# First layer's attention output by transfers instead of turns, parts sent by GpSimd, operands sent earlier

## The chip, the cores and the metric

The kernel runs on one core of a Trainium2 chip. The metric is the device time of one execution in microseconds (us); less is better. Five engines work side by side, each through its own list of instructions in order: TensorE (PE; its weight loads are shown as PEld), VectorE (DVE), ScalarE (ACT), GpSimd (POOL) and SyncE (SP), which here only starts transfers (DMAs). They meet through semaphores: an instruction may wait until a counter has reached a value.

## What is computed

Two transformer-like layers on `x` of 4 sequences, 512 tokens and 256 channels; 16 heads of 16 channels. All in float32 at the interface.

```python
# layer 0
xm = rmsnorm(x) * (1 + scale(cond)) + shift(cond)
q, k, v = split(xm @ w_qkv); q, k = rope(q), rope(k)
o = softmax(q @ k.T * DH ** -0.5) @ v            # per head
x = o @ w_out + x
# layer 1
xn = layer_norm(x)
q, k, v = xn @ q_w + q_b, xn @ k_w + k_b, (xn @ v_w + v_b) * mask
y = softmax(q @ k.T + (1 - mask) * -1e6) @ v     # per head
h = layer_norm(y) * (1 + scale(emb)) + shift(emb)
x = x + silu(h) @ out_w + out_b
```

## The kernel before

**Groups and steps.** The attention of one layer, one sequence and four heads is a group. There are 2 x 4 x 4 = 32 groups, 0 to 15 in layer 0 and 16 to 31 in layer 1. After an opening, the kernel runs one step for each group, s = 0 to 31. A step has four key tiles (k = 0 to 3) of 128 keys each. `KEY_TILE` (L43) is the order within a tile, by which every engine's list is written (`order`, L210): for each of the four heads a score product of 128 keys by 512 queries (L538), a second product that adds the row maximum with a minus sign (L550), and a product for the row maxima of the group two steps ahead (L559); and at the tile's end the product of the tile before with the values (`values`, L576), which adds up in one bank, `ACC`. ACT takes the exponentials (L765), DVE the row maxima (L938 in layer 0, L935 in layer 1), into three banks in turn (`ND = 3`). The maxima of a group are made into two float16 parts by DVE (`negate`, L946 and L948, up to group 21) or by POOL (from group 22), turned by PE in the second tile (L584), copied by ACT (L778), and written by SP into the operand of L550 (`shift`, L1443 to L1449).

**Pieces.** All other PE work is put into the middle of tiles as pieces, by the table `PIECES` (L91 to L115): `qk` and `v` are the projections (L626, L637), `y` is the output projection of a layer (L654, two for each sequence), `turn` is a transpose of normalised tokens to channels (L611, eight 128 x 128 transposes for a pair).

**Output of a group.** In the first tile of step s the last values product of group s-1 ends. ACT copies `ACC` to `oT` (L772): rows are channels of a head (16 of every 32), and one more row holds the sum of its probabilities. In the middle of tile k = 2 PE turns `oT` (four transposes, L591) into one of the DVE's three banks, and DVE writes `1 / sum` (L960) and the product (L962) into `O`, tokens by channels (`write_output`, L951). For layer 0, when the four groups of a sequence are done, `turn f0` turns `O` back to channels by tokens (L611, source `O`), ACT copies it into `xT` (L802), and `y(0, b)` reads it.

**Parts.** Queries and keys go through HBM. POOL splits each of four chunks of a sequence (unit `pu`, 0 to 3 in layer 0, 4 to 7 in layer 1) into two float16 parts (`rope`, L1210, of five instructions in layer 0; `split`, L1198, of two in layer 1). SP sends the parts, four transfers of 128 KB for a chunk, at the steps in `PARTS_AT` (L163), and loads a group's operands (L1431) three steps ahead. In step s SP's list is: `shift(s+1)`, `operands(s+3)`, then parts. Only unit 0 has transfers from POOL in the kernel before (L1276, L1278: ten). After the ropes of sequence 1 POOL waits for the mask's transfers (`mask_in`), which SP starts in step 0 behind parts, makes the mask's rows (L1307 to L1314), and then runs the ropes of sequences 2 and 3 one behind another.

**Second layer.** `project(b)` on POOL (L1332) makes the norm's factors, the normalised tokens (L910), adds the output bias (L1337), then splits and adds the values' bias (`add_bias`, L1229). Behind it POOL makes the norm of the last stage, `turn f1` reads that in tiles 0 and 1 of step 22.

Of the kernel before, what the change touches and what calls it, by code (L numbers as in the profile page):

```python
# [12 lines left out]
P = 128  # L13
# [8 lines left out]
G = 4  # L22
# [6 lines left out]
GROUPS = LAYERS * B * NG  # L29
UNIT = 64.0  # L30
# [88 lines left out]
for _b in range(B):  # L119
    STATISTICS[5 + NG * _b, 3] = ("p1", _b, 0)  # L120
    STATISTICS[6 + NG * _b, 0] = ("p1", _b, 1)
# [32 lines left out]
for _s in range(1, GROUPS - 2):  # L154
# [8 lines left out]
PARTS_AT = {-1: ((1, 0), (1, 1)), 0: ((1, 2), (1, 3)), 2: ((2, 0), (2, 1)), 3: ((2, 2), (2, 3)),  # L163
            5: ((3, 0), (3, 1)), 6: ((3, 2), (3, 3))}
for _b in range(B):
    PARTS_AT[8 + NG * _b] = ((B + _b, 0), (B + _b, 1))
    PARTS_AT[9 + NG * _b] = ((B + _b, 2), (B + _b, 3))

# [18 lines left out]
def key_tile(s, k):  # L187

    for op, h in KEY_TILE:
# [86 lines left out]

def await_shift(engine, q, n):
# [43 lines left out]
def build(nc, x, condT, mask, tables, vecs, w_cond, w_qkv, w_out, w_qkv1, v_b, emb_w, out_w, out_b, out):  # L321
# [4 lines left out]
    with ExitStack() as ctx:  # L326
# [12 lines left out]
        m.v_aug = [sb(f"v_aug{i}", [P, KT, H, W]) for i in range(VALUES)]  # L339
        m.probs = [sb(f"probs{i}", [P, G, 512]) for i in range(KT)]  # L340
# [48 lines left out]
        m.roped = [[sb(f"roped{e}{i}", [P, 512]) for i in range(2)] for e in range(2)]  # L389
        m.parts = sb("parts", [P, 2, 4, 512], F16)  # L390
# [4 lines left out]
        m.k_dram = nc.dram_tensor("k_parts", [LAYERS * B, H, 2, 2, DH, S], F16, kind="Internal").ap()  # L395

# [8 lines left out]
        q.acc_copied = sem("acc_copied")  # L405
        q.shift_high = sem("shift_high")
# [115 lines left out]
def tensor(nc, pe, m, q):  # L522
# [71 lines left out]
    def turn_tokens(piece):  # L594
        _, kind, b, h = piece
        bank = d_free(D[piece]) if for_dve(piece) else a_free(A[piece])
        if kind == "f0":
            pe.wait_ge(q.d_done, D["output", NG * b + NG - 1] + 1)
            src = m.O[b % 2]
        else:  # L600
            n = NORMAL.index((kind, b))
            src = m.XN[n % 2]
            if h == 0 and n == 0:
                pe.wait_ge(q.ident_made, 4)
                pe.wait_ge(q.xn0_made, TPB)
            elif h == 0 and n == len(NORMAL) - 1:
                pe.wait_ge(q.xn0_made, 2 * TPB)
            elif h == 0:
                pe.wait_ge(q.xn_made, TPB * n)
# [31 lines left out]
    def tokens_out(piece):  # L641
# [3 lines left out]
        if j == 0:  # L645
            pe.wait_ge(q.late_in, 64)
            if layer:
                pe.wait_ge(q.silu_made, CT * (b + 1))
            else:
                pe.wait_ge(q.a_done, turned(USES[use]))  # L650
# [104 lines left out]
def scalar(act, m, q):  # L755
# [12 lines left out]
    def copy_output(s):  # L768
        act.wait_ge(q.values_done, KT * (s + 1))
        if s:  # L770
            act.wait_ge(q.d_made, D["output", s - 1] + 1)
        act.activation(m.oT[:, :], m.ACC, ACT.Copy).then_inc(q.acc_copied, 1)  # L772
# [7 lines left out]
    def tokens(piece):  # L780
# [20 lines left out]
        if kind == "f0":  # L801
            act.activation(to, bank, ACT.Copy).then_inc(q.a_done, 1)  # L802
# [111 lines left out]
def vector(dve, m, q):  # L914
# [35 lines left out]

    def write_output(s):  # L951
        pu, g = divmod(s, NG)
        bank = made(D["output", s]).rearrange("p (t h w) -> p t h w", t=KT, h=G)
        if g == 0 and 2 <= pu < B + 2:
            dve.wait_ge(q.a_made, turned(("f0", pu - 2)))
        if g == 0 and pu >= B + 2:
            dve.wait_ge(q.xn_made, TPB * NORMAL.index(("f1", pu - 2 - B)))
        if s:
# [180 lines left out]
    for op, *at in order():  # L1139
        if op == "max":  # L1140
            maximum(*at)
            n, j, h = at
            if (j, h) == (KT - 1, MAXED[-1]) and n not in POOL_SHIFTS:
                negate(n)
        if op == "output":
# [26 lines left out]
def gpsimd(pool, m, q):  # L1172
# [24 lines left out]

    def split(pu, i):  # L1198
# [9 lines left out]
            .then_inc(q.part_pool, 1)  # L1208

# [334 lines left out]
```

## Time and profile before

| | |
|---|---|
| median of 3 runs | 509.46 us (509.26 to 510.74) |
| the profiled execution's own time | 511.63 us |
| its span, first to last instruction | 509.8 us |
| PE, busy share of the span | 97% |
| DVE | 80% |
| ACT | 68% |
| POOL | 45% |
| mean granted TensorE clock | 1.000 |
| chain that ended last: PE, DVE | 75%, 15% |
| time before step 0; steps 1 to 4; 5; 6 to 17; 18 to 21; from 22 on | 57.7; 52.9; 16.1; 178.3; 56.5; 134.4 us |

The last line is from the first score product of each step in the timeline; step 0 itself takes 13.9 us. A PE that is busy for 97% isn't at its peak for 97%: matmuls overlap, and their ends are modelled. So the timeline of PE is read by the starts: how far the first product of one tile is from the first of the next.

### The profile page before, as it was taken

Reading aid. Unit: us, or ns where it says so; the run is one execution under the profiler, and the core shown is the slowest. Engines: PE = TensorE matmul, PEld = TensorE weight load, DVE = VectorE, ACT = ScalarE, POOL = GpSimd, SP = SyncE. Lnnn points to the kernel's source line nnn. Section 1 sums busy time; section 2 is a strip of 40 time slices with the busy share of each in tenths; the row PEclk is TensorE's granted clock in tenths of the full one; section 3 lists DMA queues with packets and bytes.
Section 4 is the critical chain, followed back from the end, with each engine's and each line's share of the span. In section 5 each row is a group of like instructions: output and inputs, shape, how many; then the busy total and the mean of one; then the engine's idle time right before and its main releaser. Section 6 shows DMA issues by size and latency. Waiting matters only on the chain.

```text
span 509.8 us, 9780 instructions
## 1 busy us (share of the span) xinstructions
PE 496.1 (97%) x3301; PEld 187.0 (37%) x3301; DVE 406.4 (80%) x1046; ACT 348.7 (68%) x684; POOL 228.8 (45%) x267
## 2 busy tenths in 40 slices
PE   7999899999999999999999999999999999999997
PEld 3554323333433245333443344333433333332234
DVE  3767887998896788967898688977899999999324
ACT  2652467768577785867768676777778778777863
POOL 6479537999361320923136330643672045005401
PEclk9999999999999999999999999999999999999999
DMA  7773356341323033111321133210341112211011
GB/s 251 197 197 124 86 163 211 112 141 43 111 67 104 13 126 124 43 44 51 116 86 44 42 104 122 68 43 2 124 125 45 43 43 84 85 44 43 2 42 41
DMA packets 42217, 45.30 MB, mean 89 GB/s; under 512 B 4324, under 2 KB 40308, under 8 KB 41912
## 3 DMA queue, kind: packets, MB, share of 16 engines
q1 hardware_dynamic: 41400, 42.06, 27.0%
q0 software_dynamic: 480, 1.31, 1.0%
q10 hardware_dynamic: 288, 1.31, 0.8%
q8 instruction: 26, 0.43, 0.3%
q14 instruction: 23, 0.19, 0.1%
HBM read 25.52 MB, written 18.87 MB: 87 GB/s over the span
## 4 chain that ended last, share of the span: by engine, by line
PE 75%; DVE 15%; issue 3%; ACT 2%; DMA 2%; POOL 1%; SPq 1%; DVEq 0%; ACTq 0%; POOLq 0%
PE bank L576 18%; PE bank L626 12%; PE bank L559 11%; PE bank L550 9%; PE bank L538 8%; DVE masked L935 6%; PE bank L637 6%; DVE row_max L938 5%; PE bank L654 5%; PE bank L591 2%; PE bank L611 2%; ACT probs L765 2%; DMA k_s<-k_parts 2%; PE bank L584 1%; PE bank L712 1%
## 5 line engine op out<-in xcount | busy, mean ns | idle before, releaser
L765 ACT ACTIVATE probs<-bank 128x512 f32<-128x512 f32 x512 | 272.8, 600 | 82.1 <-PE bank L550 80.9
L559 PE MATMUL bank<-k_s,q_s 64*128 64x512 f16 x512 | 182.8, 382 | 4.0 <-DVE row_max L938 2.5
L938 DVE TENSOR_REDUCE row_max<-bank 128x1 f32<-128x512 f32 x256 | 162.5, 684 | 28.9 <-PE bank L559 27.7
L935 DVE CUSTOM_DVE_ANT_0 masked<-bank,mask_bias 128x512 bf16<-128x512 f32 x256 | 163.3, 687 | 13.4 <-PE bank L559 12.3
L538 PE MATMUL bank<-q_s,k_s 64*128 64x512 f16 x512 | 152.1, 381 | 0.9 <-ACT v_aug L842 0.5
L550 PE MATMUL bank<-shift,kx 64*128 64x512 f16 x512 | 148.9, 376 | 0.0
L576 PE MATMUL bank<-probs,v_aug 128*17 128x512 f32 x1024 | 135.4, 598 | 0.7 <-ACT probs L765 0.7
L559 PEld LDWEIGHTS bank<-k_s,q_s 64*128 64x128 f16 x512 | 46.0, 93 | 156.1 <-DVE row_max L938 68.4
L626 PE MATMUL bank<-xT,wqkv 128*128 128x512 f32 x128 | 61.7, 612 | 0.9 <-DVE xT L1064 0.6
L550 PEld LDWEIGHTS bank<-shift,kx 64*128 64x128 f16 x512 | 46.8, 95 | 31.7
L538 PEld LDWEIGHTS bank<-q_s,k_s 64*128 64x128 f16 x512 | 31.5, 94 | 13.1 <-ACT probs L765 8.0
L1205 POOL CAST parts<-plain 128x512 f16<-128x512 f32 x16 | 9.8, 611 | 52.2 <-ACT plain L823 52.2
L626 PEld LDWEIGHTS bank<-xT,wqkv 128*128 128x128 f32 x128 | 22.2, 189 | 29.5 <-issue 26.0
L1358 POOL TENSOR_SCALAR scaled<-row_max 128x16 f32<-128x16 f32 x10 | 2.6, 259 | 64.6 <-DVE row_max L935 40.5
L637 PE MATMUL bank<-wqkv,xT 128*128 128x256 f32 x128 | 31.3, 389 | 0.0
L1193 POOL TENSOR_SCALAR spread<-moments_p 128x4 f32<-128x4 f32 x4 | 0.9, 232 | 67.0 <-DVE moments_p L973 67.0
L576 PEld LDWEIGHTS bank<-probs,v_aug 128*17 128x17 f32 x1024 | 17.9, 95 | 33.6 <-issue 15.6
L654 PE MATMUL bank<-wo,xT 128*128 128x256 f32 x112 | 27.9, 392 | 0.0
L637 PEld LDWEIGHTS bank<-wqkv,xT 128*128 128x128 f32 x128 | 23.2, 190 | 8.6 <-issue 4.1
L1240 POOL TENSOR_SCALAR v_bias<-vb_row,vecs 128x256 f32<-128x256 f32 x16 | 14.8, 927 | 23.1 <-ACT v_tmp L837 22.3
L984 DVE TENSOR_TENSOR X<-bank,X 128x512 f32<-128x512 f32 x14 | 9.6, 687 | 18.8 <-PE bank L654 18.8
L654 PEld LDWEIGHTS bank<-wo,xT 128*128 128x128 f32 x112 | 20.1, 189 | 8.1 <-DVE row_max L938 2.5
(123 smaller groups left out, 499.4 us busy)
## 6 DMA issues: line engine op xcount, KB each, us to landing
q_s<-q_parts SPq DMA_DIRECT2D x32, 256.0 KB, 2.8
k_s<-k_parts SPq DMA_DIRECT2D x32, 256.0 KB, 3.1
q_parts<-parts SPq DMA_DIRECT2D x60, 128.0 KB, 3.1
k_parts<-parts SPq DMA_DIRECT2D x58, 128.0 KB, 3.8
X<-in_x SPq DMA_DIRECT2D x4, 512.0 KB, 7.3
y<-X SPq DMA_DIRECT2D x7, 256.0 KB, 2.7
tables<-in_tables SPq DMA_DIRECT2D x4, 256.0 KB, 7.1
wc<-in_emb_w SPq DMA_DIRECT2D x1, 1024.0 KB, 6.8
```

The costliest lines, as they stand in the source:

```text
L538: nc.tensor.matmul(bank, m.k_s[slot][rows, i, keys], m.q_s[slot][rows, i, :], start=True, stop=False)
L550: nc.tensor.matmul(a_bank(m, A["score", s, k, h]), keys, m.shift[s % SHIFTS][rows, i, :], start=False, stop=True).then_inc(q.a_made, 1)
L559: nc.tensor.matmul(bank, m.q_s[slot][rows, i, queries], m.k_s[slot][rows, i, :], start=True, stop=True).then_inc(q.d_made, 1)
L576: last = nc.tensor.matmul(m.ACC[W32 * h:W32 * h + W, :], m.v_aug[pu % VALUES][:, k, G * g + h, :], m.probs[k][:, h, :], start=(k == 0), st ...
L591: last = nc.tensor.transpose(bank[:, t * P:(t + 1) * P], m.oT[:, t * P:(t + 1) * P], m.ident[:, :])
L626: last = nc.tensor.matmul(bank, m.wqkv[layer][:, k, i * P:(i + 1) * P], m.xT[use % 2][:, k, :], start=(k == 0), stop=(k == CT - 1))
L637: last = nc.tensor.matmul(bank[:, t * C:(t + 1) * C], m.xT[use % 2][:, k, at], m.wqkv[layer][:, k, 2 * C:3 * C], start=(k == 0), stop=(k = ...
L654: last = nc.tensor.matmul(bank[:, t * C:(t + 1) * C], m.xT[use % 2][:, k, at], m.wo[layer][:, k, :], start=(k == 0), stop=(k == CT - 1))
L765: act.activation(m.probs[k][:, h, :], bank, ACT.Exp, scale=1.0 if s >= B * NG else float(DH) ** -0.5)\
L935: dve.tensor_tensor_reduce(m.masked[D["max", n, k, h] % ND][:, :], bank, m.mask_bias[:, b, :], 1.0, LOWEST, ALU.add, ALU.max, to)\
L938: dve.tensor_reduce(to, bank, AX.X, ALU.max).then_inc(q.d_done, 1)
L1240: pool.tensor_scalar(m.v_bias[:, :], m.vb_row[:, :], m.vecs[:, at:at + 1], None, ALU.mult)\
```

## The change

It has three parts, all in layer 0's output and in who starts which transfers.

1. **Output.** The sixteen output turns of layer 0, its `write_output` and the four `turn f0` with their ACT copies are gone. SP sends the rows of `oT` with the sums to a small tile `sums` and the four heads' rows to `raw` (the same memory as `O`), DVE takes the reciprocals of the sums in tile k = 3 (`invert`), SP writes them to HBM and reads them back, each row repeated for 16 channels, into `inverse`, and POOL multiplies (`divide`, one 128 x 512 instruction for each half of a sequence's channels) into `xT`. The pieces move: `y(0, b)` from step 5+4b (tiles 2, 3) to 6+4b (tiles 0, 1), and what follows it by about a step; step 5 has no piece left, step 21 gets one.
2. **Parts.** POOL itself sends the parts of units 1 to 7, each behind its rope or split.
3. **SP's order.** From step 1 on it is: operands(s+3), the raw output of s-1, shift(s+1), the inverses of s-1 out and in.

The diff, cut to its core:

```diff
+LAYER = B * NG
 for _b in range(B):
-    _s = 5 + NG * _b
+    _s = 6 + NG * _b
-    PIECES[_s] = (turn("f0", _b), (), *one(y(0, _b)))
-    PIECES[_s + 1] = (_other, (), (), ())
-    PIECES[_s + 2] = (turn("p1", _b), qk(1, _b, 0), qk(1, _b, 1), qk(1, _b, 2))
-    PIECES[_s + 3] = (qk(1, _b, 3), (), v(1, _b)[:1], ())
-PIECES[20] = (qk(1, LAST, 3), (), v(1, LAST)[:1], v(1, LAST)[1:])
+    PIECES[_s] = (*one(y(0, _b)), _other, ())
+    PIECES[_s + 1] = ((), (), turn("p1", _b), qk(1, _b, 0))
+    PIECES[_s + 2] = (*one(qk(1, _b, 1, 2)), qk(1, _b, 3), ())
+    PIECES[_s + 3] = (v(1, _b)[:1], (), (), ())
+PIECES[20] = (*one(qk(1, LAST, 1, 2)), qk(1, LAST, 3), v(1, LAST)[:1])
+PIECES[21] = (v(1, LAST)[1:], (), (), ())
...
-        if op == "output" and k == 2 and s:
+        if op == "output" and k == 2 and s > LAYER:
             yield op, s - 1
+        if op == "output" and k == 3 and 0 < s <= LAYER:
+            yield "sums", s - 1
...
+    def invert(s):
+        dve.wait_ge(q.sums_in, 16 * (s + 1))
+        if s:
+            dve.wait_ge(q.inv_out, 16 * s)
+        dve.reciprocal(m.inv_sum[:, :, :, :].rearrange("p t h w -> p (t h w)"), m.sums[:, :]).then_inc(q.inv_made, 1)
...
+    def send_parts(pu, i):
+        send_part(pool, m, q, pu, i, 0, q.parts_out[i])
+        pool.wait_ge(q.part_pool, 4 * (pu - 1) + i + 1)
+        send_part(pool, m, q, pu, i, 1, q.parts_out[i])
...
+    def divide(b, c):
+        use = USES.index(("f0", b))
+        pool.wait_ge(q.output_out, group_out(NG * b + 2 * c + 1))
+        pool.wait_ge(q.inv_in[c], 32 * (b + 1))
+        await_read(pool, q, use - 2)
+        pool.tensor_tensor(m.xT[use % 2][:, c, :], m.raw[b % 2][:, c, :], m.inverse[c][:, :], ALU.mult)\
+            .then_inc(q.divided, 1)
...
             rope(b, i)
+            if b == B - 1 and i in (1, 2):
+                divide(0, i - 1)
...
     def project(b):
         rstd("p1", b)
         normal("p1", b)
+        if b < LAST:
+            divide(b + 1, 0)
...
         add_bias(b, 0)
+        if b < LAST:
+            divide(b + 1, 1)
...
     for b in range(B):
         project(b)
-    add_bias(LAST, 1)
...
     for b in range(LAST):
         negate(NG * (B + b) + 6)
+        if b == 0:
+            add_bias(LAST, 1)
...
+    def raw_output(s):
+        b, g = divmod(s, NG)
+        sp.wait_ge(q.acc_copied, s + 1)
+        if b >= 2:
+            sp.wait_ge(q.divided, normalised(b - 2, g // 2))
+        if s:
+            sp.wait_ge(q.inv_made, s)
+        sp.dma_start(m.sums[:, :], m.oT[DH::W32, :].rearrange("h (c n) -> h c n", n=KT * G)).then_inc(q.sums_in, 16)
+        first = chunk_rows(g).start
+        for h in range(G):
+            sp.dma_start(m.raw[b % 2][first + DH * h:first + DH * (h + 1), g // 2, :],
+                         m.oT[W32 * h:W32 * h + DH, :]).then_inc(q.output_out, 16)
...
     for s in range(-1, GROUPS + 2):
+        if 0 < s and exists(s + 3):
+            operands(s + 3)
+        if 0 < s <= LAYER:
+            raw_output(s - 1)
         if exists(s + 1):
             shift(s + 1)
-        if s >= 0 and exists(s + 3):
+        if s == 0:
             operands(s + 3)
-        for pu, i in PARTS_AT.get(s, ()):
-            parts(pu, i)
+        if 0 < s <= LAYER:
+            inverses_out(s - 1)
+            inverses_in(s - 1)
```

## Rows read from the trace of the kernel before

**Rows 1.** The page's first part: busy us (share of the span) and instructions.
```profile
PE 496.1 (97%) x3301; PEld 187.0 (37%) x3301; DVE 406.4 (80%) x1046; ACT 348.7 (68%) x684; POOL 228.8 (45%) x267
```
**Rows 2.** Who waited for whom: us in total, times, longest us.
```profile
PEld bank L559 <- DVE row_max L938: 68.4, 113, 1.6
PEld bank L559 <- DMA k_s<-k_parts: 2.8, 5, 0.7
```
**Rows 3.** Timeline of PE, steps 5 to 7: start us, us, what, [idle before].
```profile
124.44 0.39 PE L559 MATMUL bank<-k_s,q_s 64*128 64x512 f16 x1
...
131.29 0.39 PE L559 MATMUL bank<-k_s,q_s 64*128 64x512 f16 x1
...
132.04 1.99 PE L654 MATMUL bank<-wo,xT 128*128 128x256 f32 x8
...
136.14 0.39 PE L559 MATMUL bank<-k_s,q_s 64*128 64x512 f16 x1
...
140.55 0.39 PE L559 MATMUL bank<-k_s,q_s 64*128 64x512 f16 x1
...
147.48 0.39 PE L559 MATMUL bank<-k_s,q_s 64*128 64x512 f16 x1
...
148.23 0.66 PE L591 MATMUL bank<-ident,oT 128*128 128x128 f32 x4
...
150.55 0.39 PE L559 MATMUL bank<-k_s,q_s 64*128 64x512 f16 x1
...
153.03 0.39 PE L559 MATMUL bank<-k_s,q_s 64*128 64x512 f16 x1
```
**Rows 4.** Timeline of PE: the first tile of step 9, with a turn f0.
```profile
185.10 0.39 PE L559 MATMUL bank<-k_s,q_s 64*128 64x512 f16 x1
...
188.62 0.39 PE L559 MATMUL bank<-k_s,q_s 64*128 64x512 f16 x1
```
**Rows 5.** Timeline of DVE: maxima in a row, and the two small instructions behind them.
```profile
121.14 4.41 DVE L938 TENSOR_REDUCE row_max<-bank 128x1 f32<-128x512 f32 x7
125.59 0.68 DVE L946 TENSOR_SCALAR neg_max<-row_max 128x16 f16<-128x16 f32 x1
126.31 1.19 DVE L948 SCALAR_TENSOR_TENSOR neg_max<-row_max,neg_max 128x16 f16<-128x16 f32 x1
...
141.91 0.18 DVE L948 SCALAR_TENSOR_TENSOR neg_max<-row_max,neg_max 128x16 f16<-128x16 f32 x1
```
**Rows 6.** Groups of instructions by line: busy us, mean ns of one | idle before.
```profile
L960 DVE RECIPROCAL inv_sum<-bank 128x16 f32<-128x16 f32 x31 | 7.8, 253 | 16.2 <-PE bank L591 16.2
```
**Rows 7.** Timeline of POOL: transfers, mask, two ropes of five instructions each.
```profile
20.97 1.32 POOL L1397 DMA_DIRECT2D q_parts<-parts  x2 [4.26 <-ACT parts L872]
...
28.35 2.10 POOL L1397 DMA_DIRECT2D k_parts<-parts  x4 [1.67 <-ACT parts L872]
...
78.93 1.90 POOL L1307 TENSOR_SCALAR mask_bias<-mask_bias 128x2048 f32<-128x2048 f32 x1 [10.88 <-DMA mask_row<-in_mask]
...
83.39 1.26 POOL L1219 TENSOR_TENSOR roped<-plain,tables 128x512 f32<-128x512 f32 x1
...
89.32 1.26 POOL L1219 TENSOR_TENSOR roped<-plain,tables 128x512 f32<-128x512 f32 x1 [0.17 <-POOL parts L1227]
```
**Rows 8.** Timeline of SP's transfers in step 0.
```profile
65.62 1.36 SPq L1448 DMA_DIRECT2D shift<-shift_rows  x2
...
68.16 5.11 SPq L1397 DMA_DIRECT2D k_parts<-parts  x8
```
**Rows 9.** Timeline of PE: start of the tile of `v(1, 3)[1]`, step 20, tile 3.
```profile
360.34 0.39 PE L559 MATMUL bank<-k_s,q_s 64*128 64x512 f16 x1
```
**Rows 10.** Timeline of POOL behind it: values' bias, norm's factors, normalised tokens.
```profile
364.06 0.92 POOL L1240 TENSOR_SCALAR v_bias<-vb_row,vecs 128x256 f32<-128x256 f32 x1 [1.28 <-ACT v_tmp L837]
...
368.52 0.23 POOL L1193 TENSOR_SCALAR spread<-moments_f 128x4 f32<-128x4 f32 x1
...
369.99 4.85 POOL L910 TENSOR_SCALAR XN<-O,moments_f,rstd_f 128x256 f32<-128x256 f32 x4
```

More of the change, by code:

```diff
@@ L160 @@
 POOL_SHIFTS = list(range(22, GROUPS))
[L163 to L167, printed above, removed]
 HIGH_BEHIND = [("qk", 0, 0, 2), ("qk", 0, 0, 3), ("turn", "p0", 1, 1), ("v", 0, 0, 1)]
@@ L274, in await_read, with group_out, chunk_rows, normalised @@
         engine.wait_ge(q.d_made, D["y", layer, b, 1] + 1)
+def group_out(s):
+    return 16 * G * (s + 1)
+def chunk_rows(g):
+    return slice(G * DH * (g % 2), G * DH * (g % 2 + 1))
+def normalised(b, c):
+    return CT * b + c + 1
 def await_shift(engine, q, n):
@@ L405, in build @@
         q.acc_copied = sem("acc_copied")
+        q.output_out = sem("output_out")
+        q.sums_in = sem("sums_in")
+        q.inv_out = sem("inv_out")
+        q.inv_in = [sem(f"inv_in{i}") for i in range(CT)]
+        q.divided = sem("divided")
         q.shift_high = sem("shift_high")
@@ L596, in turn_tokens @@
         bank = d_free(D[piece]) if for_dve(piece) else a_free(A[piece])
[L597 to L609, printed above, removed]
+        n = NORMAL.index((kind, b))
+        src = m.XN[n % 2]
+        if h == 0 and n == 0:
+            pe.wait_ge(q.ident_made, 4)
+            pe.wait_ge(q.xn0_made, TPB)
+        elif h == 0 and n == len(NORMAL) - 1:
+            pe.wait_ge(q.xn0_made, 2 * TPB)
+        elif h == 0:
+            pe.wait_ge(q.xn_made, TPB * n)
         for t in range(TPB):
@@ L649, in tokens_out @@
             else:
-                pe.wait_ge(q.a_done, turned(USES[use]))
+                pe.wait_ge(q.divided, normalised(b, CT - 1))
         for t in range(2):
@@ L953, in write_output @@
         bank = made(D["output", s]).rearrange("p (t h w) -> p t h w", t=KT, h=G)
-        if g == 0 and 2 <= pu < B + 2:
-            dve.wait_ge(q.a_made, turned(("f0", pu - 2)))
+        if s == LAYER:
+            dve.wait_ge(q.inv_out, 16 * LAYER)
+        if g == 0 and pu < B + 2:
+            dve.wait_ge(q.divided, normalised(pu - 2, CT - 1))
         if g == 0 and pu >= B + 2:
             dve.wait_ge(q.xn_made, TPB * NORMAL.index(("f1", pu - 2 - B)))
-        if s:
+        if s > LAYER:
             dve.wait_ge(q.d_done, D["output", s - 1] + 1)
@@ L1144, in vector @@
                 negate(n)
+        if op == "sums":
+            invert(*at)
         if op == "output":
@@ L1382, in gpsimd @@
             .then_inc(q.last_rstd, 1)
-def send_parts(engine, m, q, pu, i):
-    for part in range(2):
-        send_part(engine, m, q, pu, i, part, q.parts_out[i])
 def send_part(engine, m, q, pu, i, part, signal):
@@ L1449, in shift, with inverses_out, inverses_in @@
                 .then_inc(q.shift_in[n % SHIFTS], 16)
+    def raw_output(s):
[10 more added lines that the diff above has]
+                         m.oT[W32 * h:W32 * h + DH, :]).then_inc(q.output_out, 16)
+    def inverses_out(s):
+        sp.wait_ge(q.inv_made, s + 1)
+        sp.dma_start(m.inv_dram[s].rearrange("h (c n) -> (h c) n", n=KT * G),
+                     m.inv_sum[:, :, :, :].rearrange("p t h w -> p (t h w)")).then_inc(q.inv_out, 16)
+    def inverses_in(s):
+        b, g = divmod(s, NG)
+        sp.wait_ge(q.inv_out, 16 * (s + 1))
+        sp.wait_ge(q.part_dve, 4)
+        if g % 2 == 0 and b:
+            sp.wait_ge(q.divided, normalised(b - 1, g // 2))
+        sp.dma_start(m.inverse[g // 2][chunk_rows(g), :], m.inv_dram[s].unsqueeze(1).broadcast_to([G, DH, S]))\
+            .then_inc(q.inv_in[g // 2], 16)
     def output(b, j):
```

20 lines of the change are left out of this document (12 added, 8 removed).

## The prediction

> **What bounds the kernel now.** I read the page's first part, then who waited for whom, then the timeline of PE, and only then those of the engines that the change loads more. PE is busy for 97% of the span and DVE for 80% [rows 1]. That alone doesn't say that PE is the bound, since the longest wait of its weight loads, 68.4 us in 113 pieces, is for a bank that a row maximum of DVE frees [rows 2]. So I read tile by tile from start to start [rows 3]. An empty tile takes 2.48 us (150.55 to 153.03). A tile with a group's output turn takes 3.07 (147.48 to 150.55). A tile with a product piece takes 4.41 (136.14 to 140.55), and with a piece and an output turn 4.85 (131.29 to 136.14). A tile with a turn f0 takes 3.52 [rows 4]. DVE needs (4.41 - 0.68) / 6 = 0.62 us for one of seven maxima in a row [rows 5], so 2.48 for the four of a tile. The reader should see that the two engines are level in an empty tile, and that PE alone sets a tile with a piece. So whatever PE loses is won, but what DVE gets on top in an empty tile is paid.
>
> **What PE loses.** Of the 16 output turns of layer 0, ten stand in tiles with a product (steps 1, 5, 7, 8, 9, 11, 12, 13, 15, 16) at 4.85 - 4.41 = 0.44 us, and six in tiles without at 3.07 - 2.48 = 0.59: 4.4 + 3.5 = 7.9 us. The four turns f0 at 3.52 - 2.48 = 1.04 give 4.2. The product pieces are as many as before, and I take them at the same price in their new tiles. Together 12.1 us.
>
> **What the earlier operands give.** PE waited for `k_s` five times, 2.8 us in all [rows 2]. The loads now start at a step's beginning instead of behind its shift. I take the wait's whole price less a part in which DVE would have held PE anyway: 2.0 us. The bounds are 0 and 2.8. For this SP has five more transfers ahead of the shift. SP's small transfers take 1.36 / 2 = 0.68 us to issue [rows 8], so five are 3.4 us; a step has at least four tiles of 2.48, 9.9 us; the shift is wanted at its end and was sent in its middle. So I cost the five, and the way of the inverses through HBM, at nothing. What hides them is half a step, some 5 us; without it each step of layer 0 would pay what is over.
>
> **What DVE keeps and gets.** A group's reciprocal stays, 0.25 us from a bank [rows 6], and I take the same from SBUF (bounds 0.15 and 0.3); the product with it goes. It now stands in tile 3, which is empty in 13 of the 16 steps (not in 7, 11 and 15). With a little slack left between the engines I take 0.2 each: +2.6. The two small instructions of `negate` come at the start of the next step's first tile. Before, that tile nearly always had a piece that hid them. After, it is empty in steps 5, 7, 11, 15 and 19. Undisturbed, the pair is 0.18 each, with the gap 0.3 to 0.4 [rows 5]; I take 0.3 in steps 7, 11, 15 and 19: +1.2. In step 5 POOL works through its ropes, and there the pair took 0.68 + 1.19 us instead [rows 5]; I take +0.8 there, between 0.3 and 1.5. These rows show that DVE's small instructions wait for POOL's. The Trainium skill (SBUF — State Buffer, Who interferes with whom) has the rule for it: a DVE instruction in a 2-port mode or with two SBUF inputs and a GpSimd one lock each other out for a whole instruction, whichever starts first. It speaks against the change, which gives POOL more work, and would put the four pairs at up to 1.5 each; that is the fourth rival. DVE's maxima read banks and aren't touched by it, and the rows of the seven maxima, made during ropes, agree.
>
> **What POOL gets.** 112 transfers and eight products. A rope takes 89.32 - 83.39 = 5.93 us, four transfers 2.10, so 0.525 each; the first pair took 1.32 [rows 7]. A rope with its transfers is then 8.03. This matters at one place. `y(0, 0)` in step 6 needs `divide(0, 1)`, which stands behind seven ropes of sequences 2 and 3 and `divide(0, 0)`. Before, the mask's work started at 78.93, behind the landing of a transfer that SP issued about 5.1 us late, for it sent eight parts first [rows 8]. Without these the mask starts at 73.9 and the first rope at 83.39 - 5.1 = 78.3. Then 7 x 8.03 + 2 x 1.26 (the price of a product like the rope's first) gives 78.3 + 56.2 + 2.5 = 137.0, with semaphores 137.3. PE: step 5 started at 124.44 [rows 3]. Steps 1 to 4 lose 0.44 + 3 x 0.59 and get 4 x 0.2, so it starts at 123.0; empty, it takes 4 x 2.48 + 0.2 + 1.0 = 11.1; and the piece stands 0.75 behind the start of step 6 (131.29 to 132.04 is that distance [rows 3]). PE is there at 134.9 and waits 2.4 us. Bounds: 0, if transfers are prepared beside POOL's other work; 7.5, if the mask doesn't come earlier. Later sequences have a step's slack or more for `divide`. A split has two of a rope's five instructions, some 2.4 us, and 4.5 with its transfers: about the 4.41 between two projections, and the operands made of it aren't loaded within four steps.
>
> **The end of layer 0's pieces.** `v(1, 3)[1]` moves to step 21, tile 0. POOL's work on it began 364.06 - 360.34 = 3.7 us behind its tile's start [rows 9, 10]. From there to the end of the normalised tokens it took 369.99 + 4.85 - 364.06 = 10.8 [rows 10], of which some 0.8 is a `negate` that now comes first; so they are ready 3.7 + 10.0 = 13.7 behind the start of step 21. The turn f1 wants them at 4.41 + 2 x 2.48 + 3.07 + 0.75 = 13.2. +0.5.
>
> **The sum.** -12.1 - 2.0 + 2.6 + 1.2 + 0.8 + 2.4 + 0.5 = -6.6. The profiled execution took 511.63 us with a span of 509.8, 2.2 more than the median; a difference carries over, so 505.0 for such an execution and 502.9 against the median of 509.46. ACT loses eight copies, which PE and DVE cover: nothing.
>
> **Rivals.** (a) POOL is in time: its sends overlap other work, or cost 0.43 us or less (28 sends stand ahead of `divide(0, 1)`; 2.4 / 28 = 0.09 less than 0.525). The wait of 2.4 is gone: 500.5, down to 499 if DVE's extras are hidden too. For it: PE and DVE pass through other waits that could delay step 6. Against: the rows show the sends one behind another.
> (b) POOL's sends are dear, the side on which it is slower than before. Without the wait the change gives 6.6 + 2.4 = 9.0; that is used up when a send costs 0.525 + (2.4 + 6.6) / 28 = 0.85 us, and beyond it the kernel is slower, at 1.1 us a send by 7 us: 516. For it: the first send in a pair took 0.78, 1.32 less 0.54 [rows 7]. Against: eight others at 0.53.
> (c) SP is late: the shift or the reciprocal's sums come behind their tile because SP's five sends or its waits for inverses take over 5 us. Then each of 16 steps pays some 0.3 us: 507.7.
> (d) DVE's pairs in the four empty tiles meet POOL at 1.5 us instead of 0.3 and the reciprocals are held too: + 4.8 and some 1: 508.7, no change that can be told.
> (e) The change doesn't do what it says for the operands, since they wait for the parts or a slot: only +2.0, inside the first case.
>
> **How the numbers follow.** The forecast with its own range of 500.5 to 505.5 has 0.52. (a) 0.18, (b) 0.10, (c) 0.10, (d) 0.10. The range leaves out (b)'s far part and the best part of (a): 499.0 to 509.0. A measurement of this kernel can tell 0.3%, 1.5 us, from no change: faster by more has 0.52 + 0.18 + most of (c) and half of (d) = 0.83; within it half of (d) and some of (c) and (b), 0.08; slower 0.09.
>
> **What would show it.** Right: steps 6 to 17 together about 172.5 to 173 us instead of 178.3; step 5 near 11; one wait of PE for POOL's `xT` in step 6 of 1 to 4 us; POOL's transfers at 0.53 each; no wait for `k_s` from step 21 on. Wrong: a wait in step 6 above 7 us, such waits in steps 10, 14 or 18, empty tiles of layer 0 at 2.8 or more, or waits of PE for the shift's transfer.

## The result, and the profile after

| | before | after |
|---|---|---|
| median on the same chips | 510.73 us (508.70 to 511.51, 20 runs) | 508.68 us (507.03 to 510.78, 20 runs) |
| ratio, with its 95% interval | 1 | 0.9967 (0.9955 to 0.9979) |
| profiled execution; its span | 511.63; 509.8 us | 507.94; 506.1 us |
| mean granted TensorE clock | 1.000 | 0.997 |

The change makes the kernel faster by 0.33%, 1.7 to 2.1 us, where 6.6 were forecast. The direction was right, the size was not. That 508.68 us lies inside the forecast's wide range, 499.0 to 509.0, is luck: the kernel before had 509.46 us as the median of 3 runs and has 510.73 of 20, and the slow end of the range stood for SP's list and DVE's pairs, which turn out not to be the cause. The two profiled executions differ by 3.7 us in their spans, more than the medians do, for that of before lay 0.9 us above its median and that of after 0.7 us under its own. So the profiles below explain 3.7 us, of which some 1.6 us is the luck of two executions. One of the executions below, 1164.7 us of the kernel bestm, was in a slow state and is left out of its ratio.

The first part of the page after: busy us (share of the span) and instructions, the granted clock in tenths over 40 slices, the queues that POOL's transfers use, and the shares of the chain that ended last.
```profile
PE 486.6 (96%) x3205; PEld 177.7 (35%) x3205; DVE 397.9 (79%) x1030; ACT 343.6 (68%) x676; POOL 301.4 (60%) x387
...
PEclk9999999999989999999999999999999999999999
...
q0 software_dynamic: 7904, 16.03, 10.5%
...
PE 66%; DVE 20%; DMA 4%; issue 4%; POOL 3%; ACT 2%; SPq 1%; DVEq 0%; POOLq 0%; ACTq 0%
```
Against [rows 1], PE and DVE have lost 9.5 and 8.5 us of work and POOL has got 72.6. The chain's share of POOL has gone from 1 to 3%, and one slice in which the granted clock isn't full is new. Both lead to one place, which the waits name: us in total, times, longest us.
```profile
PE bank L676 <- POOL xT L1294: 4.7, 1, 4.7
...
PE bank L585 <- DVE row_max L961: 2.7, 9, 0.7
...
PE bank L576 <- DMA shift<-shift_rows: 0.9, 1, 0.9
```
The longest wait of PE is now for POOL's second `divide` in step 6. The timeline of PE there (start, length, what, [idle before]), from the start of step 6 over its first tiles to step 7:
```profile
133.72 0.39 PE L585 MATMUL bank<-k_s,q_s 64*128 64x512 f16 x1
...
139.27 3.59 PE L676 MATMUL bank<-wo,xT 128*128 128x256 f32 x8 [4.73 <-POOL xT L1294]
...
144.53 0.39 PE L585 MATMUL bank<-k_s,q_s 64*128 64x512 f16 x1
...
155.87 0.39 PE L585 MATMUL bank<-k_s,q_s 64*128 64x512 f16 x1
```
The tile takes 144.53 - 133.72 = 10.81 us where one with a piece takes 4.41. The product behind the wait takes 3.59 us; the same one took 1.99 in the kernel before [rows 3]. So the wait cost 4.73 us of idle time and about 1.6 us more behind it: 6.4 in all.

The lengths of the stages, from the first score product of one step to that of another, as in the table of before; "forecast" is the sum of the prediction's own terms that fall into the stage, with two product pieces (3.9 us) that go from step 5 to step 18 and come out at nothing.

| stage | before | after | forecast | measured |
|---|---|---|---|---|
| steps 1 to 4 | 52.9 | 51.7 | -1.4 | -1.2 |
| step 5 | 16.1 | 10.4 | -4.3 | -5.7 |
| steps 6 to 17 without the wait | 178.3 | 171.4 | -6.4 | -6.9 |
| the wait in step 6 and what follows it | 0 | 6.4 | +2.4 | +6.4 |
| steps 18 to 21 | 56.5 | 60.6 | +4.2 | +4.1 |
| from step 22 on | 134.4 | 134.0 | -1.0 | -0.4 |
| sum | | | -6.5 | -3.7 |

One term is off by 4.0 us, more than the whole miss of the profile pair (2.9 us); the others together came out 1.2 us better than forecast.

### The profile page after: what moved, and what is told of

It is laid out like the page before. It is cut to its first block, busy times and chain, and to the rows that moved or that the text cites. A ratio compares the mean times of both kernels' runs of the same rounds, so it can differ in the third digit from the quotient of the medians.

```text
span 506.1 us, 9691 instructions
## 1 busy us (share of the span) xinstructions
PE 486.6 (96%) x3205; PEld 177.7 (35%) x3205; DVE 397.9 (79%) x1030; ACT 343.6 (68%) x676; POOL 301.4 (60%) x387
## 4 chain that ended last, share of the span: by engine, by line
PE 66%; DVE 20%; DMA 4%; issue 4%; POOL 3%; ACT 2%; SPq 1%; DVEq 0%; POOLq 0%; ACTq 0%
PE bank L602 16%; PE bank L585 11%; PE bank L648 9%; DVE masked L958 9%; PE bank L576 8%; PE bank L564 8%; PE bank L676 5%; DVE row_max L961 5%; PE bank L659 5%; DMA tables<-in_tables 2%; ACT probs L787 1%; PE bank L633 1%; DMA X<-in_x 1%; PE bank L617 1%; DMA k_parts<-parts 1%
## 5 line engine op out<-in xcount | busy, mean ns | idle before, releaser
L1449 POOL DMA_DIRECT2D q_parts<-parts x60 | 34.8, 585 | 4.9 <-ACT parts L895 4.0
L1449 POOL DMA_DIRECT2D k_parts<-parts x62 | 35.0, 570 | 3.3 <-ACT parts L895 3.3
L676 PE MATMUL bank<-wo,xT 128*128 128x256 f32 x112 | 29.5, 409 | 4.7 <-POOL xT L1294 4.7
L676 PEld LDWEIGHTS bank<-wo,xT 128*128 128x128 f32 x112 | 21.2, 199 | 13.3 <-issue 6.0
```

Of the source, the lines that this page charges most:

```text
L676: last = nc.tensor.matmul(bank[:, t * C:(t + 1) * C], m.xT[use % 2][:, k, at], m.wo[layer][:, k, :], start=(k == 0), stop=(k == CT - 1))
L1449: engine.dma_start(to, m.parts[:, part, i, :]).then_inc(signal, 16)
```

## The experiments

The lines of these kernels can be a few apart from those of after; what an instruction does is the same. Each ratio is against the kernel before, run on the same chip between the others (medians 510.7 to 511.0 us).

### again: the kernel after, once more

> The changed kernel once more, for times on the same chip as its variants and a second trace. Its first trace has a span 3.7 us under that of before (506.1 against 509.8), the medians of the two kernels lie 2.05 us apart (508.68 against 510.73). If the wait in step 6 is steady from execution to execution, this trace shows it again at 4.7 us within 0.5, with the first output product at half the granted clock, and the ratio to before is near 0.997. If the wait comes and goes, the step 6 of this trace differs by 1 us or more.

Median 509.29 us, ratio 0.9979 (0.9960 to 0.9999), span 507.0. The wait is there again, and with its slow product:
```profile
139.56 3.75 PE L676 MATMUL bank<-wo,xT 128*128 128x256 f32 x8 [6.08 <-POOL xT L1294]
```
In the first profile of after, step 4 had lost 1.3 us to a late shift. Here it hadn't (its first tile 4.41 us, not 5.68), and PE waited 1.35 us longer instead; the product starts at 139.56, as against 139.27. So until step 6 POOL sets the time: what PE loses or wins in steps 1 to 5 doesn't count in this kernel. The expectation of 4.7 us within 0.5 for the wait was missed; it is the time at which it ends that is steady.

### early: the divide that PE waits for, one chunk of ropes earlier

```diff
-            if b == B - 1 and i in (1, 2):
-                divide(0, i - 1)
+            if b == B - 1 and i == 1:
+                divide(0, 0)
+                divide(0, 1)
```


> Both halves of divide for sequence 0 run behind POOL's rope of chunk 1 of sequence 3, instead of behind chunk 1 and chunk 2; nothing else differs. The second half is then done at 128.8 + 1.3 + 1.2 = 131.3 us instead of 139.1, before PE wants it at 134.5. Theory 1 (the missing gain was lost where PE waited for POOL in step 6, 4.7 us, and then ran the product at the lower clock, 1.6 us): step 6's first tile falls from 10.81 to about 4.4, and the kernel is 6.3 us faster than the changed one, near 502. Theory 2 (the transfers made something else dear that stays): the wait goes, but the time moves by less than 3 us.

Median 502.04 us, ratio 0.9840 (0.9817 to 0.9864), span 498.4, clock 1.000. The product starts without a wait and at its old length:
```profile
133.37 1.99 PE L676 MATMUL bank<-wo,xT 128*128 128x256 f32 x8
```
Step 6 takes 15.75 us instead of 22.15, 6.4 less, and the median is 6.6 lower than that of after, 7.25 lower than that of again on the same chip. That is the experiment which decides: the wait with what follows it is the gain that is missing. The profiled execution, 500.20 us, is the fastest of the five, and POOL happened to begin with the mask at 75.42 us in it instead of 77.15; the next trace has the same result without that. Once more under another name, since another kernel was to be compared with it:

> The kernel with the early divide again, for times beside its two descendants on the same chip: 0.984 of before within 0.0025, 502 us, as the first time, with no wait of PE for POOL in step 6.

502.29 us (501.93 to 502.52), ratio 0.9841 (0.9822 to 0.9859): the same. The mask's work began at 78.03 us, and the first tile of step 6 is 4.41 us again. Step 4 has the late shift of the first profile of after (its first tile 5.71 us), and since nothing waits for POOL behind it, here its 1.3 us are paid.

### busy: products that nobody reads while PE waits

Behind the first tile's products and ahead of the wait, PE makes 22 products of a zero tile into the bank that `y(0, 0)` then overwrites.
```diff
             else:
+                if b == 0:
+                    keep_busy(22, bank)
                 pe.wait_ge(q.divided, normalised(b, CT - 1))
```


> PE runs 22 products on zeros (0.21 us each, 4.7 us) into the bank of the first output product of sequence 0 before it waits for POOL; their result is overwritten. Theory 1 with the clock: the wait as such stays (the product can't start before 139.3), but the granted clock stays at full, the product's eight matmuls take 2.0 us instead of 3.6, and the kernel gains 1.6 us on the changed one. Rival (the lower clock at the product has another reason, or the 3.6 us come from reading what POOL has just written): the product still takes 3.6 us and the time is that of the changed kernel.

Median 506.79 us, ratio 0.9930 (0.9911 to 0.9949). The wait for POOL stays where it was, but the product behind it is fast. Timeline of PE in busy:
```profile
133.59 4.92 PE L704 MATMUL bank<-idle 128*128 128x512 f16 x22
...
139.64 2.00 PE L678 MATMUL bank<-wo,xT 128*128 128x256 f32 x8 [1.13 <-POOL xT L1296]
```
And the stretch from 139 to 143 us in three kernels (window, length; busy us and instructions of PE, PEld, DVE, ACT, POOL; granted clock; share and GB/s of the DMA engines), first again, then busy, then early:
```profile
139.00:143.00 4.00, 3.44 (x8) 2.53 (x8) 0.00 (x0) 0.00 (x0) 3.92 (x4) 0.50 0.15 56
```
```profile
139.00:143.00 4.00, 3.36 (x22) 1.78 (x22) 1.33 (x3) 0.79 (x2) 3.92 (x4) 1.00 0.24 88
```
```profile
139.00:143.00 4.00, 4.00 (x29) 1.63 (x28) 3.39 (x7) 2.10 (x5) 3.78 (x4) 1.00 0.33 96
```
The granted clock is 0.50 of full behind an idle PE, the lower of the two levels (1.2 and 2.4 GHz), and 1.00 behind a PE that had worked. The operand was as freshly written by POOL as before, so the rival in the expectation is out. In after, 1.6 us of the 6.4 are the clock's and the rest is the wait's. In again step 6 takes 24.00 us, 8.2 more than in early, of which 6.08 is the wait; its first tile takes 12.66 us against 10.47 in busy, so there the clock cost 2.2 us, 1.75 of it in the product. That the clock falls after idle time is also what the Trainium skill says (TensorE: Matmul & The Clock Gate, The HAM clock gate); its table has the same two levels.

### mask: the mask's transfers sent ahead of step 0

```diff
-        if s == 0:
+        if s == -1:
             sp.dma_start(m.mask_bias[:, :, :], m.mask.rearrange("b t -> (b t)").partition_broadcast(P))\
                 .then_inc(q.mask_in, 16)
             sp.dma_start(m.mask_row[:, :], m.mask).then_inc(q.mask_in, 16)
+        if s == 0:
```


> The changed kernel with the two transfers of the mask sent a step earlier, behind the shift of group 0. POOL's mask work then starts when DVE's third maxima are made, at about 73.3 us, instead of at 77.15, and all that stands behind it on POOL, divide(0, 1) too, is 3.9 us earlier: done at 135.2 instead of 139.1. Theory 1: PE's wait in step 6 falls from 4.7 to 6.1 us to 1 to 2, the clock stays at full, so 5.4 us are won on the changed kernel. Rival (the wait's size isn't set by when POOL starts, or the late landing moves to something else): less than 2 us.

Median 504.73 us, ratio 0.9884 (0.9864 to 0.9904), span 503.3. POOL's work on the mask begins at 73.41, the time that the prediction had put in, and the first tile of step 6 falls to 4.73 us. It is 4 us less than after, not 5.4. The profiled execution shows 3.8 us that were lost elsewhere. Step 4 has a late shift: PE waits 1.6 us for it, and the first tile takes 6.40 us instead of 4.41. And from the start of the last tile to the end it takes 17.90 us instead of 16.08, all of it behind the last instruction of PE and DVE, where only transfers of `y` are under way. The second `divide` is done at 135.30 us and PE is there at 135.8. Without the late shift PE would be there some 2 us earlier, and about 1.5 us of the wait would be left (an estimate from these numbers), which is what was expected. So part of the wait is gone here because PE is late. Timelines of POOL and PE in mask:
```profile
73.41 1.89 POOL L1359 TENSOR_SCALAR mask_bias<-mask_bias 128x2048 f32<-128x2048 f32 x1 [3.04 <-DVE neg_max L971]
```
```profile
110.68 0.39 PE L576 MATMUL bank<-shift,kx 64*128 64x512 f16 x2 [1.60 <-DMA shift<-shift_rows]
```

### order: the kernel before, with only the operands ahead of the shift

```diff
+        if 0 < s and exists(s + 3):
+            operands(s + 3)
         if exists(s + 1):
             shift(s + 1)
-        if s >= 0 and exists(s + 3):
+        if s == 0:
             operands(s + 3)
```


> The kernel before with one edit: from step 1 on SP loads the operands of s+3 ahead of the shift of s+1. Nothing of the output or of the parts' senders changes. The forecast took 2.0 us for this (bounds 0 and 2.8, from five waits for k_s). By the first trace of the changed kernel only the waits in the first tiles of steps 7, 23 and 27 are gone (0.64 + 0.46 + 0.27 us), those of 25 and 29 stay at 2.81 us, so they weren't waits that this lifts: -1.4 us, 509.3. Rival: nothing, since DVE holds PE there anyway.

Median 509.90 us, ratio 0.9977 (0.9965 to 0.9989): -1.2 us. By steps, step 7 gains 0.64 us, step 23 0.45 and step 27 0.27, together 1.4. Of the two other waits, one is in step 26 (0.26 us at 424.33 of the kernel before), whose length is 12.23 us with it and 12.17 without. The fifth, 0.61 us at 36.57, lies in the opening, ahead of step 0, where nothing has changed, and stays. Steps 25 and 29, which the expectation names, have no wait for `k_s` in the trace of before. In exchange order waits 0.93 us for `k_s` at 88.16, in step 2, where before didn't; steps 2 and 3 together are as long as before, 24.01 us against 23.93.

### pool: order, and the parts of units 1 to 7 sent by POOL

```diff
     def split(pu, i):
...
+        send_parts_pool(pu, i)
...
     def rope(b, i):
...
+        send_parts_pool(b, i)
...
-        for pu, i in PARTS_AT.get(s, ()):
-            parts(pu, i)
```


> The kernel before with the same new order of SP's loads, and with POOL sending the parts of units 1 to 7 (108 transfers and more behind its ropes and splits); output turns as before. Theory 1 (POOL's sends cost only what waits for POOL): nothing in this kernel waits for POOL's later ropes within a step's slack, so it is like the one with the new order alone, -1.4 us, within 1 us of it. Theory 2 (POOL's sends hold up DVE's small instructions or the other transfers in every step): slower than that by 2 us or more, and the steps 1 to 6 show it.

Median 510.36 us, ratio 0.9996 (0.9987 to 1.0005), about 1 us slower than order, with intervals that just overlap. The traces show it in one tile, the first of step 7 (4.81 us instead of 3.51), where the turn of sequence 0 wants POOL's normalised tokens. Timeline of PE in pool:
```profile
153.39 1.06 PE L611 MATMUL bank<-ident,XN 128*128 128x128 f32 x8 [1.26 <-POOL XN L910]
```
From step 8 on each step is as long as in order to 0.01 us. There POOL's sends thus cost nothing but where something waits for POOL. (The spans of the two profiled executions stand the other way round, 508.0 and 508.9, because steps 2 to 5 took 2.0 us less in that of pool; the ratio, over eleven executions, decides.)

### spparts: the kernel after, with the parts sent by SP as before

SP sends the parts behind the shift and ahead of the inverses of its step; in layer 1 in steps 9+4b and 10+4b, since the pieces come a step later.
```diff
         if s == 0:
             operands(s + 3)
+        for pu, i in PARTS_AT.get(s, ()):
+            parts(pu, i)
         if 0 < s <= LAYER:
             inverses_out(s - 1)
...
     def split(pu, i):
...
-        send_parts(pu, i)
...
     def rope(b, i):
...
-        send_parts(b, i)
```


> The changed kernel with its second part undone: SP sends the parts of units 1 to 7 again, behind a step's shift and ahead of the inverses. POOL is free of 28 sends of 0.53 us ahead of divide(0, 1). Theory 1: no wait for POOL in step 6, 6.3 us won there; but SP's list is longer by 5.1 us in two of four steps, so that loads, sums and shift come later, and the steps with a late shift pay about 1.3 us each as step 4 did in the changed kernel: 500 to 510 in all. Theory 2 (POOL's sends cost by contention in every step): it is faster by more than 6.3 us. Theory 3 (SP's list is the scarce thing, which is why POOL sends): it is slower than the changed kernel.

Median 508.12 us, ratio 0.9955 (0.9934 to 0.9975), so not to be told from after. The wait in step 6 is gone, its first tile at 4.41 us, 6.4 less. But SP is now the one that is late. A timeline of SP in step 3, and of PE in step 4, both of spparts:
```profile
95.30 5.89 SPq L1453 DMA_DIRECT2D q_parts<-parts  x8
```
```profile
113.34 0.39 PE L582 MATMUL bank<-shift,kx 64*128 64x512 f16 x2 [2.62 <-DMA shift<-shift_rows]
...
113.87 3.00 PE L665 MATMUL bank<-wqkv,xT 128*128 128x256 f32 x8
```
And the window from 115 to 118 us, columns as above:
```profile
115.00:118.00 3.00, 3.00 (x11) 1.25 (x9) 0.55 (x1) 0.00 (x0) 2.78 (x4) 0.50 0.73 205
```
SP issues eight parts for 5.9 us, and the list behind them, ending with the shift of step 4, comes late: PE waits 2.62 us, and the product that follows takes 3.00 instead of 1.99, since the granted clock falls to the lower level again, 0.50. Steps 2 and 4 lose 1.75 and 3.4 us against after. The end is 2.1 us longer too, but mask, whose SP sends no more than after, had 1.8 us there as well, so that isn't put down to this edit. With the wait in step 6 gone and SP late, the time is 6 us above early: in this place of SP's list the parts cost about as much as they save on POOL. Whether another place in the list would do wasn't tried.

### evp: early, and a values piece moved from step 6+4b to the empty tile of step 7+4b

```diff
-    PIECES[_s] = (*one(y(0, _b)), _other, ())
-    PIECES[_s + 1] = ((), (), turn("p1", _b), qk(1, _b, 0))
+    PIECES[_s] = (*one(y(0, _b)), (), ())
+    PIECES[_s + 1] = (_other, (), turn("p1", _b), qk(1, _b, 0))
```


> The kernel with both halves of divide early, and with the piece of v(1, b-1)[1] (for b = 0: v(0, 3)[1]) moved from tile 2 of step 6+4b to tile 0 of step 7+4b. In the changed kernel tiles 0 and 1 of steps 7, 11, 15 and 19, which are empty and meet DVE's two small instructions, take 5.50, 5.66, 5.78 and 5.41 us, 0.4 to 0.8 over two undisturbed ones of 2.48. If those instructions in an empty tile are the cause (the forecast's +0.3 each was that term, too small), a product in tile 0 hides them and the four batches give 0.5 to 0.7 each back: 2 to 2.6 us less than with the early divide alone, about 499.7. Rival (the tiles are long because two empty ones follow each other): no gain, since then the empties lie elsewhere.

Median 503.21 us, ratio 0.9854 (0.9841 to 0.9868): by the medians 1 us more than early, within the noise of the two, where 2 to 2.6 less were expected. The pair of `negate` is hidden, as expected: tiles 0 and 1 of steps 7, 11, 15 and 19 take 4.41 + 2.51. But tile 3 of steps 6, 10 and 14 rises from 2.47 to between 3.44 and 3.50, and tiles 2 and 3 of step 18, the first of them without a piece now, take 3.47 and 3.13. Each pair of steps is 0.2 to 1.2 us longer than in early. Timeline of DVE there in evp:
```profile
143.88 0.74 DVE L999 BATCH_NORM_STATS2 stats<-X 128x6 f32<-128x256 f32 x2
144.66 0.38 DVE L1004 BATCH_NORM_AGGREGATE moments_p<-stats 128x2 f32<-128x6 f32 x4
144.95 2.45 DVE L961 TENSOR_REDUCE row_max<-bank 128x1 f32<-128x512 f32 x4
147.32 0.24 DVE L978 RECIPROCAL inv_sum<-sums 128x16 f32<-128x16 f32 x1
```
The piece had hidden the statistics of layer 0's output, 1.1 us of DVE, which now lie in two tiles without a product. A piece is a cover, and this one was worth no less where it stood. The expectation's rival, that two empty tiles in a row are long by themselves, is answered by step 9 of after: its three empty tiles take 2.51, 2.47 and 2.47 us.

### best, bestm and bestm2: the parts put together

best is early with two further edits; bestm and bestm2, the same kernel, have the mask's transfers in step -1 too. The first edit moves the four `kx` transfers from step 2 to step 7, the second one the values' bias behind the norm that `turn f1` reads.
```diff
-        if s == 2:
+        if s == 7:
             sp.wait_ge(q.mask_step, 4)
...
-        if b == 0:
-            add_bias(LAST, 1)
         rstd("f1", b)
         normal("f1", b)
+        if b == 0:
+            add_bias(LAST, 1)
```


> Early divide, and two more edits: SP's four transfers of the mask's rows into kx come at the end of step 7 instead of step 2, and POOL's values' bias for v(1, 3)[1] comes behind the tokens of turn f1 instead of ahead of them. If the late shift of step 4 (0 or 1.3 us in the changed kernel's two traces, 2.0 in the one with the early mask) comes from SP standing at those transfers, step 4's first tile is 4.41 in this trace; and the first tile of step 22 falls from 3.5 to 3.1. Together 0.4 us for sure and 0 to 2 more: 0.4 to 1.5 us less than the early divide alone. Rival: something else takes their place and the time stays.

Median 501.48 us, ratio 0.9829 (0.9811 to 0.9848), 0.8 us less than early on the same chip (502.29), as expected. The first tile of step 22 is back at 3.09 us, and that of step 4 takes 4.41. Against that tile 2 of step 7 takes 4.57 instead of 3.51. Timelines of PE and of POOL in best:
```profile
155.82 1.06 PE L633 MATMUL bank<-ident,XN 128*128 128x128 f32 x8 [1.01 <-ACT probs L787]
```
```profile
150.82 4.85 POOL L933 TENSOR_SCALAR XN<-X,moments_p,rstd_p 128x256 f32<-128x256 f32 x4
```
The wait is put down to ACT, but the turn starts 0.15 us behind the end of what it reads, `XN` (150.82 + 4.85 = 155.67): it was POOL again.

> As the one with three edits, and the mask's two transfers a step earlier. With the divide early nothing of PE waits for POOL's ropes any more, so an earlier start of the ropes of sequences 2 and 3 is worth nothing: within 1 us of the kernel with three edits. Rival (POOL's start still matters): 1 us less or more.

Median 499.92 us, ratio 0.9794 (0.9771 to 0.9816). This kernel was run once more, and its profile is read from that run:

> The kernel with four edits again, for a trace: its time was 499.9 us, 1.5 us under the kernel with three edits, where I had expected no difference over 1 us. The trace of the three-edit kernel has 4.57 us for the third tile of step 7, which holds turn p1 and takes 3.51 undisturbed: PE waits there for POOL's normalised tokens. If POOL's lateness is what the mask's earlier transfers take away, this trace has that tile at 3.5 us and the time is near 500 again. Rival: the tile stays at 4.5, and the gain is elsewhere (steps 2 to 5).

Median 499.49 us (499.32 to 500.07), ratio 0.9782 (0.9769 to 0.9795), span 497.5. That is 1.5 and 2.0 us under best, where at most 1 had been expected. The two lines above, in bestm2:
```profile
153.93 1.09 PE L633 MATMUL bank<-ident,XN 128*128 128x128 f32 x8
```
```profile
148.61 4.86 POOL L933 TENSOR_SCALAR XN<-X,moments_p,rstd_p 128x256 f32<-128x256 f32 x4
```
POOL's list is 2.2 us earlier and that of PE waits for it nowhere: tile 2 of step 7 takes 3.51. With the mask earlier POOL has slack at two places, not at one. That is less than half of the gain: up to the end of step 7 this trace is 2.2 us ahead of that of best, of which step 7 gives 0.9 and steps 2 to 5 give 1.2, the place that the expectation's rival named. What gives it there, in the first tiles of steps 3 and 5, wasn't tested; such tiles differ by as much between two traces of one kernel. This version beats both kernels, the one before by 2.2%.

## Where the prediction was right, and the step that failed

**What PE loses: right.** The product tiles take 4.40 to 4.45 us and the empty ones 2.47, as read from [rows 3]. Step 5 alone fell by 5.7. With the wait out of the way, in early, the kernel is 8.6 us faster than before; the prediction's sum without its wait is 9.0.

**The wait in step 6: the mechanism right, the size wrong, and it is the step that failed.** The term +2.4 measured +6.4, for two reasons: the prediction let the mask land as much earlier as its transfers start, and it priced the wait at its length alone. It had the mask's work at 73.9, the second `divide` ready at 137.0 and PE there at 134.9. In the profile of after they are 77.15, 139.1 and 134.5. POOL's own stretch was even shorter than forecast, 139.13 - 77.15 = 62.0 us instead of 63.1; a rope with its sends took 89.49 - 81.61 = 7.9 instead of 8.03. Timeline of POOL, then SP's two transfers of the mask, both of after:
```profile
77.15 1.91 POOL L1359 TENSOR_SCALAR mask_bias<-mask_bias 128x2048 f32<-128x2048 f32 x1 [6.91 <-DMA mask_row<-in_mask]
...
81.61 1.28 POOL L1259 TENSOR_TENSOR roped<-plain,tables 128x512 f32<-128x512 f32 x1
...
89.49 1.28 POOL L1259 TENSOR_TENSOR roped<-plain,tables 128x512 f32<-128x512 f32 x1
...
137.85 1.28 POOL L1294 TENSOR_TENSOR xT<-O,roped 128x512 f32<-128x512 f32 x1
```
```profile
68.09 0.46 SPq L1564 DMA_DIRECT2D mask_bias<-in_mask  x1
68.60 0.34 SPq L1566 DMA_DIRECT2D mask_row<-in_mask  x1
```
```profile
68.11 2.12 POOL L1449 DMA_DIRECT2D k_parts<-parts  x4
```
The mask's large transfer (1 MB, `mask_bias`) started 5.2 us earlier, at 68.09 instead of 73.31, and the small one behind it at 68.60 instead of 73.94, but POOL began at 77.15 instead of 78.93: 9.1 us from the issue of the large one, not 5.6. I had moved the start and kept the landing time; the forecast's bound of 7.5 us for the wait stood for just that, the mask not coming earlier. The first of the two in the kernel before:
```profile
73.31 0.59 SPq L1482 DMA_DIRECT2D mask_bias<-in_mask  x1
```
The windows of after (columns as above) show how full the DMA engines were all that time, with the kernel's loads behind the mask's on SP and four of POOL's parts, issued at 68.11, beside it:
```profile
68.00:70.00 2.00, 2.00 (x20) 0.55 (x19) 2.00 (x4) 1.21 (x3) 2.00 (x5) 1.00 0.78 255
70.00:72.00 2.00, 2.00 (x18) 0.52 (x16) 2.00 (x4) 1.82 (x4) 0.24 (x1) 1.00 0.93 126
...
74.00:76.00 2.00, 2.00 (x17) 0.36 (x16) 1.29 (x2) 1.63 (x3) 0.00 (x0) 1.00 0.99 400
76.00:78.00 2.00, 2.00 (x25) 0.74 (x21) 1.58 (x3) 1.87 (x4) 0.85 (x1) 1.00 0.99 378
```
In the kernel before the engines were no less full while the mask was under way (a share counts a packet in the window in which it starts, so it can pass 1):
```profile
74.00:76.00 2.00, 2.00 (x17) 0.39 (x18) 1.29 (x2) 1.63 (x3) 0.00 (x0) 1.00 1.07 259
76.00:78.00 2.00, 2.00 (x25) 0.72 (x21) 1.62 (x3) 1.90 (x4) 0.00 (x0) 1.00 0.91 329
```
So the engines' share alone doesn't tell why it took longer. The other runs narrow it down. In pool, which has POOL's sends and the new order of the loads but none of the new output, the mask was issued at 68.03 and POOL began at 77.41, 9.4 us later. In spparts, with the parts back on SP, it was issued at 73.31 and POOL began at 79.08, 5.8 us. The other traces with POOL's sends have 7.3 (early) to 9.7 us (early2). So the longer way came with the second part of the change: the mask issued 5 us earlier, and four of POOL's parts at the same moment. Which of the two does it, and how, stays open. What mask shows is that with POOL's start at 73.41 the `divide` is done at 135.30 instead of 139.13. The mask came 3.2 us late and PE 0.4 early, POOL's stretch gave 1.1 back: 2.4 + 3.2 + 0.4 - 1.1 = 4.9, measured 4.73. For the later sequences the prediction gave `divide` a step's slack or more; there was less, 4.1 to 4.7 us (done at 193.53, wanted at 197.62 in step 10), and it sufficed.

**The clock: missing from the sum.** A wait was priced at its length, with nothing for what follows it. The product behind it took 1.6 us more, and busy shows that this goes away when PE works through the wait. It is also why early gained 6.4 in the step and not 4.7.

**DVE.** The reciprocal, 0.24 us, cost nothing: in the thirteen steps where 0.2 each had been put in, 2.6 in all, tile 3 is as long as an empty one was before, 2.47 us in all but step 2, where it has another piece and takes 3.48 as against 3.47. An empty tile has that much slack. The pair of `negate` cost more: tiles 0 and 1 of steps 7, 11, 15 and 19 take 5.50, 5.66, 5.78 and 5.41 us, 2.5 more than eight empty tiles, where 1.2 was put in. In step 5 it was the other way round, 0.28 + 0.17 us instead of the 0.68 + 1.19 of [rows 5], hence the better step 5. Timeline of DVE in step 7 of after:
```profile
155.18 1.82 DVE L961 TENSOR_REDUCE row_max<-bank 128x1 f32<-128x512 f32 x3
157.03 0.17 DVE L969 TENSOR_SCALAR neg_max<-row_max 128x16 f16<-128x16 f32 x1
157.24 0.33 DVE L971 SCALAR_TENSOR_TENSOR neg_max<-row_max,neg_max 128x16 f16<-128x16 f32 x1
```
Together 3.8 was forecast and 2.5 measured. Rival (d), 1.5 us for a pair, didn't come. The prediction called it shown by [rows 5] that DVE's small instructions wait for POOL's; the rows show that they were long, not what they waited for. The first tiles of steps 2, 3 and 5 do vary from trace to trace, between 2.47 and 3.42 us in after and early; that this is DVE meeting POOL wasn't tested.

**The operands: too much.** 1.4 us instead of 2.0, the same three places in after and in order. Of the five waits one gave 0.06 of its 0.26 us and one lies ahead of step 0, where the new order doesn't reach.

**POOL's sends: right for the ropes.** 2.12 us for four, 0.53 each; behind a split they take 2.38 to 2.52, 0.60 to 0.63 each, at places where nothing waits for them. Rival (b) didn't come. Its bound of 0.85 us a send was added up wrongly, since the 6.6 already held the wait of 2.4: the gain is used up at 0.525 + 6.6 / 28 = 0.76 us, and 1.1 us a send would make the kernel 9.5 us slower than before, not 7. What they cost is a question of who waits for POOL, and pool showed a second such place (step 7) that the list of the prediction didn't have.

**The turn f1: right.** Step 22 begins with a tile of 3.5 instead of 3.09 us, and best took the loss away by the reordering that this cause asks for.

**SP: wrong in one execution of two.** The five sends were costed at nothing. In the first profile of after the shift of step 4 came 0.88 us late and the tile took 1.27 more; in again it didn't. That is rival (c), in one step instead of sixteen, and in after it cost nothing since PE had to wait in step 6 anyhow; in early2 and mask it did cost. Why it is late in some executions isn't settled: with the `kx` transfers in step 2 it was late in three traces (after, early2, mask) and not in four (again, early, busy, evp), and in the two with them moved to step 7 it wasn't, which two traces can't decide.

**The checks.** The forecast named steps 6 to 17 at 172.5 to 173 us; its own terms give 178.3 - 6.4 + 2.4 = 174.3, so that line was added up wrongly. Measured were 177.8. The wait of 4.73 was above the 1 to 4 us named as right and below the 7 named as wrong; a wait for the shift's transfer, another sign of being wrong, came once.

## What to carry to other kernels

When work moves to an engine with slack, list every place at which a busy engine waits for the receiving one, and price a wait of some us with the time by which the next TensorE work is slower behind it. A transfer that is issued earlier doesn't keep its time to landing: see what else is issued at that moment, and put the old landing into the range as a bound. A large gain can hide behind one instruction that stands a few places too late in a list: the same change with one `divide` moved was worth four times as much.

## What the runs showed of the hardware

- Behind 4.7 and 6.1 us of idle time PE's granted clock was at the lower level, and eight matmuls took 3.59 and 3.75 us instead of 1.99. With 22 products of zeros in the wait (4.92 us) and 1.13 us of idle time they took 2.00. In spparts 2.62 us of idle time was followed by 3.00 us for a like product, and the clock was at the lower level between 115 and 118 us, after PE had been at work again since 113.34. In mask a product behind 1.60 us of idle time took 1.99.
- What waited for a 1 MB transfer began 9.1 us behind its issue in after, 9.4 in pool and 7.3 in early, with four of POOL's transfers issued beside it, and 5.6 in the kernel before and 5.8 in spparts, without them, with the DMA engines about equally full: 78 to 99% in after, 91 to 107% in before.
- POOL spends 0.53 to 0.63 us on each 128 KB transfer of its own, during which its other work stands still; SP issues eight of them in 5.9 us, 0.74 each, in spparts.
